# First attention: the row maxima of a group by query half instead of by head pair, and the first group's first units between its own looks

## The reference

```
q, k, v = x @ Wq.T, x @ Wk.T, x @ Wv.T      # 32 heads of 8, rotary on q and k
scores  = q @ k.T / sqrt(8)
scores += bias[h, i - j]  for 0 <= i - j < 128;  -inf for j > i
m       = max(max_j scores, offset[h])
p       = exp(scores - m)
out     = (p @ v) / (sum_j p + exp(offset[h] - m)) @ Wo.T
```

## Time and profile before

| | |
|---|---|
| runs | 1083.94 us median of 3 (1083.74 to 1088.75) |
| profiled execution | 1085.72 us, span 1083.9 us |
| TensorE busy | 976.4 us (90%) |
| VectorE busy | 751.0 us (69%) |
| ScalarE busy | 577.4 us (53%) |
| GpSimd busy | 398.9 us (37%) |

### The profile page before, as it was taken

The page is one execution under the profiler, slowest core; times in us unless marked ns, Lnnn a source line. Parts: engine busy times, 40 slices in busy tenths (PEclk is TensorE's granted clock), DMA queues, the critical chain, the costliest instruction groups (busy, mean ns, idle before and its releaser), DMA issues. The chain is left out here.

```text
span 1083.9 us, 20902 instructions
## 1 busy us (share of the span) xinstructions
PE 976.4 (90%) x7872; PEld 669.5 (62%) x7896; DVE 751.0 (69%) x1865; ACT 577.4 (53%) x1167; POOL 398.9 (37%) x261
## 2 busy tenths in 40 slices
PE   4999677999999998989989879999999999999697
PEld 3787423333444343678867657777777777777585
DVE  7756976889888982254577657767777776777644
ACT  6442403666766677543355446555556555555264
POOL 3011220045423550000045036555656555566155
PEclk9999857999999999989989999999999999999899
DMA  4020434235532401022010000000000000000001
GB/s 108 1 81 27 153 66 85 45 71 95 97 71 62 95 23 60 1 78 78 1 40 0 1 1 1 2 1 2 2 2 2 2 2 2 1 2 2 1 1 40
DMA packets 25182, 37.94 MB, mean 35 GB/s; under 512 B 3000, under 2 KB 20904, under 8 KB 23560
## 3 DMA queue, kind: packets, MB, share of 16 engines
q1 hardware_dynamic: 25080, 36.59, 14.4%
HBM read 30.53 MB, written 5.85 MB: 34 GB/s over the span
## 5 line engine op out<-in xcount | busy, mean ns | idle before, releaser
L812 POOL TENSOR_SCALAR P<-P,rec 128x1024 f32<-128x1024 f32 (+7 forms) x128 | 220.1, 1724 | 177.2 <-DVE rec L1858 177.2
L936 ACT ACTIVATE PT<-bank 128x512 f32<-128x512 f32 (+2 forms) x320 | 153.0, 552 | 86.8 <-PE bank L1291 80.4
L1717 DVE CUSTOM_DVE_ANT_0 bank<-bank,stripS 128x128 f32<-128x128 f32 (+1 forms) x224 | 129.3, 606 | 29.3 <-PE bank L1229 29.3
L1443 PE MATMUL pair<-KH,QH 128*128 128x512 f16 (+3 forms) x576 | 116.1, 329 | 16.5 <-ACT P L1005 13.8
L1005 ACT ACTIVATE P<-pair,nm 128x1024 f32<-128x1024 f32 (+7 forms) x128 | 95.5, 746 | 56.0 <-DVE nm L1837 56.0
L1484 PE MATMUL bank<-PT,VH 128*128 128x128 f16 x1728 | 117.2, 219 | 0.1
L1229 PE MATMUL bank<-KT,QT 96*128 96x128 bf16 (+1 forms) x336 | 104.4, 338 | 10.5 <-DVE MX L1717 5.4
L1484 PEld LDWEIGHTS bank<-PT,VH 128*128 128x128 f16 x1728 | 107.0, 98 | 2.9 <-DVE PT L1866 0.2
L1866 DVE TENSOR_TENSOR PT<-bank,PT 128x384 f16<-128x384 f32 (+1 forms) x192 | 99.7, 547 | 11.6 <-ACT PT L820 11.6
L1274 PE MATMUL bank<-QT,KT 128*128 128x512 bf16 (+3 forms) x360 | 93.2, 326 | 13.7 <-ACT PT L936 5.6
L1632 DVE TENSOR_TENSOR hf<-sil,bank 128x512 f32<-128x512 f32 x64 | 44.0, 687 | 88.8 <-PE bank L1077 66.1
(11 more groups left out here) (181 smaller groups left out, 1951.1 us busy)
## 6 DMA issues: line engine op xcount, KB each, us to landing
KT<-qk_dram SPq DMA_DIRECT2D x21, 192.0 KB
stripS<-band_rows SPq DMA_DIRECT2D x28, 128.0 KB, 3.0
qk_dram<-parts SPq DMA_DIRECT2D x12, 256.0 KB, 2.3
stripT<-seq_dram SPq DMA_DIRECT2D x27, 88.0 KB, 8.6
q_raw<-w_gu SPq DMA_DIRECT2D x4, 512.0 KB, 10.7
w_raw<-w_dense SPq DMA_DIRECT2D x2, 1024.0 KB, 7.0
w_raw<-w_q SPq DMA_DIRECT2D x2, 1024.0 KB, 5.5
QT<-qk_dram SPq DMA_DIRECT2D x14, 128.0 KB
```

The costliest lines, as they stand in the source:

```text
L812: pool.tensor_scalar(rows, rows, rec1[:, m % 4:m % 4 + 1], None, ALU.mult).then_inc(s["pn"], 1)
L936: act.activation(PT[:, n % 4, hs[0]:hs[-1] + 1, 0:ni], src, ACT.Exp).then_inc(s["s2_exp"], 1)
L1443: ins = pe.matmul(out, QH1[:, h % 2, l, P * ib:P * (ib + 1)], KH1[:, r, h // (H1 // GR), HALF * c:HALF * c + nj], start=(i == 0), stop=(i ...
L1717: dve.tensor_tensor_reduce(out, out, stripS[:, h, HALF - nj:HALF], 1.0, LOWEST, ALU.add, ALU.max, mx).then_inc(s["s1_max"], 1)
```

## The change

- `maxima(g, half)` now means half of the queries and all four heads: four transposes of 12 rows for eight of 6, a copy of 12 x 512 for 6 x 1024, four row transfers (one for each head, 512 columns) for two.
- Looks of later groups take query blocks 0 to 3 of all heads first, then blocks 4 to 7 head by head.
- Unit 0 waits for the first half's rows, unit 4 for the second half's. The first maxima of group g+1 are turned after unit 8 of group g, the second after unit 0 of group g+1.
- Group 0: the first maxima follow pair 7. From pair 8 on pairs use two double banks, and after pair 13 the remaining ten alternate with the score tiles of units 0 to 3, which use banks 4 and 6 alone. Six looks of group 1 follow, with the second maxima after two of them, then unit 4. `LEAD` is 0.
- SP issues the second half's rows at the start of a group, ahead of the loads, and the first half's after the quantiser's output. Group 1's loads come after the first rows of group 0.

```diff
-        MT3 = z("MT3", [3 * GH // 2, 2, S], BF16)
+        MT3 = z("MT3", [3 * GH, 2, S], BF16)
...
-        LOOK1 += [(g, h, k) for g in range(1, NG) for h in range(GH) for k in range(N1)]
+        LOOK1 += [(g, h, k) for g in range(1, NG) for lo, hi in ((0, 4), (4, N1)) for h in range(GH) for k in range(lo, hi)]
...
+        def half_done(g, half):
+
+            return at_look1[(g, GH - 1, (3, N1 - 1)[half])] + 1
...
-        LEAD, LEAD_FIRST = 16, 12
-        PER_UNIT = [[5, 4, 3, 3, 5, 5, 5, 5, 5, 5, 4, 3]]
+        LEAD, LEAD_FIRST, EARLY_PAIRS = 0, 6, 14
+        PER_UNIT = [[0, 0, 0, 0, 6, 6, 6, 6, 5, 5, 4, 4]]
         PER_UNIT += [[5, 4, 3, 2, 5, 5, 5, 5, 5, 4, 3, 2]] * (NG - 1)
...
-        FIRST_TURNS = {PAIRS.index((0, N1 - 1)) + 2: 0}
-        TURNS = {1: ("o", -1, 1), 3: ("m", 1, 0), 5: ("o", 0, 0), 8: ("m", 1, 1)}
+        TURNS = {0: ("m", 0, 1), 1: ("o", -1, 1), 5: ("o", 0, 0), 8: ("m", 1, 0)}
...
+        FIRST_TILES = first2[4]
...
-            return bank[SCORE_BANKS[i2 % 4]]
+            return bank[SCORE_BANKS[2 + i2 % 2 if i2 < FIRST_TILES else i2 % 4]]
+
+        def pair_of(n):
+            return pair[n % 3 if n < 8 else n % 2]
...
             def maxima_rows(g, half):
                 sp.wait_ge(s["m_ev"], 2 * g + half + 1)
-                for i in range(2):
-                    sp.dma_start(queries(g)[ROWS:ROWS + 3, 2 * half + i, :], MT3[3 * i:3 * i + 3, half, :]).then_inc(m_in[half], 16)
+                for h in range(GH):
+                    sp.dma_start(queries(g)[ROWS:ROWS + 3, h, HALF * half:HALF * (half + 1)], MT3[3 * h:3 * h + 3, half, 0:HALF]).then_inc(m_in[half], 16)
...
+            maxima_rows(0, 0)
             load_group(1)
-            maxima_rows(0, 0)
-            maxima_rows(0, 1)
             for g in range(NG):
+                maxima_rows(g, 1)
                 if g + 2 < NG:
                     load_group(g + 2)
...
                 for half in range(2):
+                    if half and 1 <= g < 7:
+                        sp.wait_ge(s["q_ops"], QUANT_OPS * g)
+                        sp.dma_start(q_dram[g - 1], q_lo[:, :]).then_inc(s["q_out"], 16)
+                    if half and g + 1 < NG:
+                        maxima_rows(g + 1, 0)
                     for h in range(2 * half, 2 * half + 2):
                         if g + 2 < NG:
                             strip_first(GH * (g + 2) + h)
-                    if half and 1 <= g < 7:
-                        sp.wait_ge(s["q_ops"], QUANT_OPS * g)
-                        sp.dma_start(q_dram[g - 1], q_lo[:, :]).then_inc(s["q_out"], 16)
-                    if g + 1 < NG:
-                        maxima_rows(g + 1, half)
...
-                copy(MT3[:, half, :], ring_bank(("m", g, half)).bitcast(BF16)[0:3 * GH // 2, :]).then_inc(s["m_ev"], 1)
+                copy(MT3[:, half, 0:HALF], ring_bank(("m", g, half)).bitcast(BF16)[0:3 * GH, 0:HALF]).then_inc(s["m_ev"], 1)
...
+                        if g == 0 and u == 3:
+                            maxima(0, 1)
...
-                elif n >= 3:
+                elif 3 <= n < 8:
                     pe.wait_ge(s["s1_max"], 2 * (n - 2))
+                elif n >= 8:
+                    pe.wait_ge(s["s1_max"], 2 * (n - 1))
...
-                if u == 0 and k == 0:
-                    for half in range(2):
-                        pe.wait_ge(m_in[half], 32 * (g + 1))
-                if i2 >= 4:
+                if UNITS2[u][1] == 0 and k == 0:
+                    pe.wait_ge(m_in[UNITS2[u][0]], 16 * GH * (g + 1))
+                if i2 < 2:
+                    pe.wait_ge(s["s1_max"], 16)
+                    pe.wait_ge(s["m_ev"], 1)
+                elif i2 < FIRST_TILES:
+                    pe.wait_ge(s["s2_exp"], i2 - 1)
+                elif i2 < FIRST_TILES + 2:
+                    pe.wait_ge(s["s1_max"], GH * N1)
+                else:
                     pe.wait_ge(s["s2_exp"], i2 - 3)
...
-                for tb in range(TB):
-                    src = M3[:, tb, 2 * half:2 * half + 2, :].rearrange("p h q -> p (h q)")
-                    ins = pe.transpose(to[0:3 * GH // 2, P * tb:P * (tb + 1)], src, identb[:, :])
+                for b in range(4):
+                    src = M3[:, 4 * half + b, :, :].rearrange("p h q -> p (h q)")
+                    ins = pe.transpose(to[0:3 * GH, P * b:P * (b + 1)], src, identb[:, :])
                 ins.then_inc(s["m_tr"], 1)
...
+            def first_units():
+
+                n = EARLY_PAIRS
+                for u in range(4):
+                    for k in range(len(score_tiles(u))):
+                        look2(0, u, k)
+                        if k % 2:
+                            look2_bands(0, u, k - 1, k + 1)
+                        if n < len(PAIRS):
+                            look1_pair(n)
+                            n += 1
+                    values(u - 1)
+                for i in range(LEAD_FIRST):
+                    if i == 2:
+                        maxima(0, 1)
+                    look1(GH * N1 + i)
+
             def attention():
-                for n in range(len(PAIRS)):
+                for n in range(8):
                     look1_pair(n)
-                    if n in FIRST_TURNS:
-                        maxima(0, FIRST_TURNS[n])
-                for i in range(GH * N1, GH * N1 + LEAD_FIRST):
-                    look1(i)
-                maxima(0, 1)
+                maxima(0, 0)
+                for n in range(8, EARLY_PAIRS):
+                    look1_pair(n)
+                first_units()
                 for g in range(NG):
-                    for u in range(NU):
+                    for u in range(0 if g else 4, NU):
...
-                if k == N1 - 1 and h % 2:
-                    maxima(g, h // 2)
+                if h == GH - 1 and k in (3, N1 - 1):
+                    maxima(g, int(k != 3))
...
-                dve.wait_ge(s["eo"], 2 * g + 2)
+                dve.wait_ge(s["eo"], 2 * g + w + 1)
```

More of the change, by code:

```diff
@@ L435, in build @@
             RING += [("s", i, 0)]
+        RING.insert(2, ("m", 0, 1))
         for g in range(NG):
@@ L443, in ring_bank @@
         def ring_bank(use):
-            if use[0:2] == ("m", 0):
-                return bank[6 + use[2]]
+            if use == ("m", 0, 0):
+                return bank[6]
             return bank[RING_BANKS[at_ring[use] % 3]]
@@ L914, in maxima @@
                 if g:
-                    act.wait_ge(m_in[half], 32 * g)
-                copy(MT3[:, half, :], ring_bank(("m", g, half)).bitcast(BF16)[0:3 * GH // 2, :]).then_inc(s["m_ev"], 1)
+                    act.wait_ge(m_in[half], 16 * GH * g)
+                copy(MT3[:, half, 0:HALF], ring_bank(("m", g, half)).bitcast(BF16)[0:3 * GH, 0:HALF]).then_inc(s["m_ev"], 1)
                 act.wait_ge(s["m_ops"], M_OPS * (2 * g + half + 1))
@@ L919, in maxima @@
                     act.wait_ge(s["den"], 4 * (g - 2) + 3)
-                heads = slice(2 * half, 2 * half + 2)
-                act.activation(EO[:, g % 2, :, heads], mt[2][:, :, heads], ACT.Exp).then_inc(s["eo"], 1)
+                tok = slice(4 * half, 4 * half + 4)
+                act.activation(EO[:, g % 2, tok, :], mt[2][:, tok, :], ACT.Exp).then_inc(s["eo"], 1)
             def attention():
-                for half in range(2):
-                    maxima(0, half)
+                maxima(0, 0)
                 for g in range(NG):
@@ L1247, in look1_pair @@
                 for i in range(2):
-                    ins = pe.matmul(pair[n % 3][:, HALF * i:HALF * i + nj], queries(0)[0:ROWS, h0 + i, P * ib:P * (ib + 1)], KT3[0:ROWS, 0, h0 + i, j0:j0 + nj],
+                    ins = pe.matmul(pair_of(n)[:, HALF * i:HALF * i + nj], queries(0)[0:ROWS, h0 + i, P * ib:P * (ib + 1)], KT3[0:ROWS, 0, h0 + i, j0:j0 + nj],
                                     start=True, stop=True, skip_group_check=True)
@@ L1256, in look1_pair @@
                             first = STRIP_ROWS * (3 - q) + 2 * P - w
-                            ins = pe.matmul(pair[n % 3][STRIP_ROWS * q:STRIP_ROWS * (q + 1), HALF * i + nj - w:HALF * i + nj], flipb[:, :],
+                            ins = pe.matmul(pair_of(n)[STRIP_ROWS * q:STRIP_ROWS * (q + 1), HALF * i + nj - w:HALF * i + nj], flipb[:, :],
                                             stripT[:, 1, h0 + i, first:first + w], start=False, stop=True, skip_group_check=True)
@@ L1286, in look2_bands @@
                     for k, hs in enumerate(score_tiles(u)):
+                        if not first_k <= k < last_k:
+                            continue
                         for j, h in enumerate(hs):
@@ L1726, in maximum_pair @@
                 dve.wait_ge(s["s1"], 2 * n + 2)
-                src = pair[n % 3][:, :].rearrange("p (h j) -> p h j", h=2)[:, :, 0:nj]
+                src = pair_of(n)[:, :].rearrange("p (h j) -> p h j", h=2)[:, :, 0:nj]
                 dve.tensor_reduce(MX[:, 0, ib, h0:h0 + 2, slot], src, AX_X, ALU.max).then_inc(s["s1_max"], 2)
-                if k == N1 - 1:
```

(21 more changed lines are left out.)

17 lines of the change are left out of this document (7 added, 10 removed).

## The result

The changed kernel takes 1095.88 us (median of 4, 1093.94 to 1097.06), the kernel before 1086.05 beside it (1083.74 to 1088.75): ratio 1.0083, 95% interval 1.0061 to 1.0105. It is slower by 0.8%, where I forecast 0.8% faster with 13% for slower, and 1095.9 lies outside the range. The profiled execution has a span of 1093.4.

What follows compares the result with a forecast made beforehand. TensorE was taken to bound a full group, busy 32.96 of 35.2 us. Terms -7.4 + 3.7 - 3.4 - 1.2 = -8.3 us gave 1075.6 us from the median of 1083.94, range 1066 to 1087.

Steps and rivals of the forecast that it cites:

- Steps 1 to 5: Start of the attention, up to unit 4 of group 0: in effect at 178.5 against 185.89, -7.4 us.
- the term for the clock: Ahead of unit 4 of group 0: TensorE's idle time may mean 3 us at half speed, costing 1.5 us.
- step 5: From the end of pair 23 to unit 4: about 7.7 us, then 1.5 us for possible half clock.
- early-clock rival: Start of the attention: fuller TensorE mixture brings full clock by 156, unit 4 at 173.3, total 1070.4; chance 0.19.
- Step 6: From unit 4 of group 0 on: 21 more looks at 0.176 us, +3.7 us, in group 6 and five in group 0.
- Step 7: Turns of maxima from unit 4 on: four transposes for eight save 0.28 us each, -3.4 us.
- Step 8: TensorE's waits in each group, with the maxima moved: 0.2 us saved per group, -1.2 over six, bounds -3 and +4.
- Step 9: Looks by query half, the wide ones together: VectorE at most 93% busy, cost 0, at most 0.5 us per group.
- Step 10: DMAs and GpSimd's last quantiser steps: later group loads and steps ending 1 us later cost 0.
- late rows: Query rows' DMAs in every group: held 5 us longer, they stop TensorE and the time is 1094.5; chance 0.14.

Runs made afterwards that it cites:

- moved wait: The changed kernel with GpSimd's sixth quantiser operation, not its seventh, waiting for the next group's first-half maxima: 1076.81 us, ratio 0.992 to the kernel before.
- before, wait moved too: The kernel before with GpSimd's wait for the first-half maxima put ahead of its third quantiser operation: 1078.96 us, ratio 0.9931.

## Why the prediction was wrong

All on one footing, in us from the first pair's reduction on VectorE (132.4 before, 135.5 after, read in each trace), to the first exp of the unit named and to the last exp of the attention:

| | unit 4 of group 0 | group 1 | group 7 | last exp |
|---|---|---|---|---|
| before | 54.4 | 79.4 | 287.9 | 313.0 |
| after | 45.8 | 74.4 | 298.8 | 324.0 |
| after, moved wait | 45.6 | 74.4 | 280.1 | 305.3 |
| before, wait moved too | 54.2 | 79.2 | 281.7 | 306.9 |

The forecast was -8.3 at the last exp. The changed kernel has +11.0; with the conflict gone it has -7.7, and 1076.8 us for 1075.6 forecast (from 1083.94; the kernel before beside this run had 1086.21). That these come so close is in part luck, as steps 6 to 9 show.

- **Steps 1 to 5, the start: right.** Unit 4 is 8.6 earlier in this table; forecast was 8.9 before the term for the clock. Inside, the first transposes came 0.8 late, mostly because of the cast, and pair 23 ended at 170.3 on the axis of before for 169.3 forecast; the way from there to unit 4 took 7.4 for 7.7. The clock rose at 171.1, at 168.0 on the axis of before, for 166 to 169 forecast. It fell again at 181.4 for 3.4 us, as step 5 allowed. The early-clock rival falls: in 157 to 161 TensorE is shown 4.00 of 4.00 us busy and the clock is 0.50 (rows in the last section).
- **Step 6, the looks: right in group 6, too low in group 0.** With the conflict gone from both, group 6 takes 34.0 us where the kernel before takes 31.4: 2.6 for 16 looks, forecast 2.8. In group 0, though, a look costs 0.37 and not 0.176 (the run with twelve looks behind the pairs). By group 1, 5.0 us of lead were left, where the terms of steps 5 to 7 give about 6.8.
- **Step 7, the transposes: the saving is there and doesn't reach the period.** The period with the moved wait is 34.3, and steps 7 and 8 gave 35.2 - 0.56 - 0.2 = 34.4, but by luck. TensorE is busy 0.46 less than in the kernel before with its wait moved, for 0.56 forecast, and idle 0.57 more. What shortens the period is the conflict: 1.0 us where step 8 had 0.2.
- **Step 8, the waits: this one failed.** It said that the quantiser's seventh operation waits for the first-half maxima, "so they don't meet there either". The sixth operation has no such wait, and the prediction worked out no time for it. By the pace of before it ends 12.6 us into the group (294.87 less 282.3), so maxima after that would have met nothing. But the 16 looks ahead of the maxima are the narrow ones, as step 9 itself says, and VectorE was done with them 10.9 us into the group; GpSimd started its chain 0.7 later than before (288.08 for 284.5, 285.20 for 282.3). The sixth operation and the first cast now start within 0.1 of each other. The size was beyond my bound too: +4 over six groups, where the moved wait took 18.7 us out of the attention, from 324.0 to 305.3. Of 3.1 per group, 1.8 is TensorE's wait (2.82 for 1.02) and the rest the clock that the wait costs: group 3, which kept it, took 36.1, the others 37.3 and more. The Trainium skill, "SBUF — State Buffer", Who interferes with whom, says that a VectorE instruction with two SBUF inputs meets a GpSimd instruction that reads SBUF, and that the one that comes first keeps the shared ports for its whole instruction while the other is blocked. The trace agrees: 295.83 + 1.97 is the end of the sixth. For the casts it agrees only in part: the second cast of the kernel before was let go 1.69 us ahead of the end of the 2.80 us operation, in all six groups. I had used this page for the casts alone.
- **Step 9, the order of the looks: 0 was too low.** TensorE's waits for VectorE are 1.89 us a group with the moved wait, 0.48 in the kernel before with its wait moved; since waits on exps shrink, 0.57 more idle time is left, a little over the bound of 0.5. It eats what step 7 saves. Whether the wide looks in a row make it or the new places of the maxima was not tried.
- **Step 10: right**, the later loads cost nothing that shows.

The slower case I named, late rows, was the wrong mechanism with the right shape: a stop of TensorE in every group. That its 1094.5 lies close to the 1095.9 measured is chance.

What the change is worth by itself: both kernels with the conflict taken away differ by 1.6 us in the table and by 2.2 in the medians (1076.81 and 1078.96), and their intervals overlap, so the run times don't show that the change gains anything. 6.1 of the 7.7 us come from the moved wait, which the kernel before could have had alone. The earlier start gives 5 us at group 1 and the missing lead of looks takes 3.2 back by group 7 (205.7 from group 1 to 7, for 202.5).

## What to carry to other kernels

When work moves to another time, ask on every engine what runs beside it at its new place, above all a two-input or cast operation of VectorE beside a wide one of GpSimd: a small operation can take the big one's length. A wait that looks like a data dependency may be a guard against just this; find what it guards and move it with the work. Then a stop longer than the buffers cover can cost twice on TensorE, once itself and once by the clock, as it did here in five groups of six. And when two kernels differ in several terms, take the same disturbance out of both before saying which term was right: a sum can come out by luck.

## What the runs showed of the hardware

- A 16-column VectorE operation held by a 1024-column one of GpSimd ends 0.03 to 0.04 us after it (297.80 for 297.77; 264.00 for 263.96; 266.22 for 266.19), whether cast or subtraction. The first cast of the kernel before keeps to this (287.84 for 287.80). The second doesn't: it starts 0.20 after a one-input operation of 2.80 us (L752) and ends at 289.01, 1.69 ahead of its end. Why is open.
- GpSimd's fill (no input) held a cast as well, 0.84 us for 0.18, until 144.58 where the fill ended at 144.54.
- 96-row matmuls in pairs, and pairs mixed with score tiles, left the clock at half while TensorE was shown fully busy (145 to 149 before; 157 to 161 after); the full clock came at 171.1, after the first V products at 168.7. What of the mixture decides was not tried. The table by stretch of the changed kernel (PE, PEld, DVE, ACT, POOL busy, PEclk, DMA, GB/s):

```profile
157.00:161.00 4.00, 4.00 (x30) 0.94 (x30) 2.57 (x3) 1.08 (x2) 0.00 (x0) 0.50 0.32 59
169.00:173.00 4.00, 4.00 (x39) 1.12 (x32) 1.75 (x2) 0.30 (x1) 0.00 (x0) 0.73 0.00 0
...
181.00:185.00 4.00, 4.00 (x20) 1.53 (x19) 2.67 (x11) 2.42 (x5) 0.00 (x0) 0.57 0.78 155
```

- With a TensorE wait of 2.8 to 3.0 us the clock fell to half for 3.4 us or more in five of the six groups that had one, and not in group 3 (2.82 us, clock 1.00 throughout); with the wait of 1.02 us in each of groups 1 to 6 of the moved wait it never did.
